# Four row buffers and two moved steps in the last stage of a graph network kernel on one Trainium2 core

## The reference, cut to what matters

```python
proj = (x @ gat_w.T).reshape(n, NH, FOUT)                 # NH 4, FOUT 64
e = jax.nn.leaky_relu(s_src[src] + s_tgt[tgt], 0.2)
exp_e = jnp.exp(e - jnp.max(e))
agg = segment_sum(proj[src] * attn[:, :, None], tgt)      # attn = exp_e / denom[tgt]
...
xc, z = jnp.split(xs @ in_proj_w.T, 2, axis=-1)           # xs: the nodes in order of degree
xc = silu(conv over 4 nodes of xc)
dbc = xc @ x_proj_w.T
dt = softplus(dbc[:, :16] @ dt_proj_w.T + dt_proj_b)
h_t = exp(dt * A) * h_(t-1) + (dt * xc) * B               # 256 channels x 16 states
y = (h @ C + xc * D_param) * silu(z) ; y @ out_proj_w.T
```

## Time and profile before

| what | value |
|---|---|
| median of 3 runs | 8897.01 us (8894.12 to 8900.41) |
| the profiled execution, its own time | 8896.2 us |
| its span | 8894.4 us |
| mean granted clock of PE | 0.724 |
| busy in the span: PE, DVE, ACT, POOL | 52%, 54%, 14%, 58% |
| the last stage | about 6391 to 8387 us of the span |

### The profile page before, as it was taken

How to read it: one execution, slowest core, us unless ns; L and a number is a source line. 1 busy time by engine, 2 the same in 40 slices (tenths; PEclk the granted TensorE clock), 3 DMA queues, 4 the chain that set the end, 5 groups by cost and what they waited for, 6 DMA issues and landing times. The chain is left out here.

```text
span 8894.4 us, 95573 instructions
## 1 busy us (share of the span) xinstructions
PE 4623.8 (52%) x18992; PEld 3629.7 (41%) x18993; DVE 4836.3 (54%) x11590; ACT 1231.8 (14%) x2744; POOL 5163.8 (58%) x4985
## 2 busy tenths in 40 slices
PE   4008244544457777656666555545454555554354
PEld 3002133333356666644444344433344444444333
DVE  9462388888822222245455344444466666666644
ACT  1002011111101111100000000001122222222111
POOL 0021366766667777677777677777655556555400
PEclk6557677677778888877777677777677777667676
DMA  0201256555423333233333233333222332222200
GB/s 8 75 16 52 59 143 170 161 159 162 130 80 94 92 90 94 69 84 99 92 95 95 63 83 96 89 92 92 75 85 83 91 91 83 86 86 80 71 6 9
DMA packets 485777, 772.81 MB, mean 87 GB/s; under 512 B 296031, under 2 KB 316310, under 8 KB 481979
## 3 DMA queue, kind: packets, MB, share of 16 engines
q0 software_dynamic: 265504, 666.90, 27.1%
q10 hardware_dynamic: 19838, 70.21, 2.1%
q1 hardware_dynamic: 200345, 34.81, 2.1%
HBM read 822.37 MB, written 46.03 MB: 98 GB/s over the span
## 5 line engine op out<-in xcount | busy, mean ns | idle before, releaser
L794 POOL DMA_INDIRECT gat_rows<-scratch_gat,gat_index x1856 | 1857.4, 1001 | 576.3 <-issue 540.0
L1071 PE MATMUL gat_ps<-gat_work,k_ident 128*128 128x256 f32 x3712 | 1214.3, 500 | 933.2 <-DVE gat_work L865 817.6
L1645 POOL DMA_INDIRECT m_rows<-scratch_gat,m_index x928 | 1097.1, 1182 | 861.0 <-DVE m_work L1934 581.5
L1071 PEld LDWEIGHTS gat_ps<-gat_work,k_ident 128*128 128x128 f32 x3712 | 941.3, 260 | 1213.2 <-issue 900.4
L794 POOL DMA_INDIRECT conv_rows<-scratch_kv,conv_index x928 | 931.9, 1004 | 410.7 <-issue 267.6
L1071 PE MATMUL conv_ps<-conv_work,k_ident 128*128 128x256 f32 x1856 | 668.4, 538 | 851.2 <-DVE conv_work L865 779.5
L1211 POOL DMA_INDIRECT rel_rows<-scratch_x,rel_index x928 | 926.7, 999 | 286.5 <-issue 273.8
L1071 PEld LDWEIGHTS conv_ps<-conv_work,k_ident 128*128 128x128 f32 x1856 | 511.8, 283 | 1008.2 <-issue 821.2
L1698 PE MATMUL m_ps<-m_work,k_ident 128*128 128x256 f32 x1664 | 524.2, 487 | 359.2 <-DVE m_work L1934 359.2
L1443 PE MATMUL rel_ps<-rel_factor,rel_rows 128*128 128x128 f32 x3712 | 581.6, 330 | 214.6 <-DMA rel_rows<-scratch_x,rel_index 214.6
L1443 PEld LDWEIGHTS rel_ps<-rel_factor,rel_rows 128*128 128x128 f32 x3712 | 563.2, 244 | 226.8 <-DMA rel_rows<-scratch_x,rel_index 154.5
(11 more groups left out here) (453 smaller groups left out, 7840.3 us busy)
## 6 DMA issues: line engine op xcount, KB each, us to landing
m_bc<-scratch_bc ACTq DMA_DIRECT2D x25, 2048.0 KB, 8.6
gat_rows<-scratch_gat,gat_index POOLq DMA_INDIRECT x1856
conv_rows<-scratch_kv,conv_index POOLq DMA_INDIRECT x928
rel_rows<-scratch_x,rel_index POOLq DMA_INDIRECT x928
m_rows<-scratch_gat,m_index POOLq DMA_INDIRECT x928
scratch_runs<-e_runs_sb SPq DMA_DIRECT2D x1, 12890.6 KB
scratch_kv<-p_row ACTq DMA_DIRECT2D x25, 256.0 KB
gat_index<-scratch_slots SPq DMA_DIRECT2D x232, 4.0 KB, 1.8
```

Source lines behind the costliest of these rows:

```text
L794: pool.indirect_dma_start(out=rows[b][:, s, :], out_offset=None, in_=table, in_offset=bass.IndirectOffsetOnAxis(ap=index[b][:, s:s + 1], a ...
L1071: ins = pe.matmul(ps_sum[min(b, 1)], ident, work[b][:, s, :], start=s == 0, stop=s == S - 1)
L1645: pool.indirect_dma_start(out=rows[b][:, s, :], out_offset=None, in_=dr["gat3"], in_offset=bass.IndirectOffsetOnAxis(ap=index[b][:, s:s + ...
```

## The change

A fourth row buffer (with index and extras buffers) is added. The first chunk of a tile now always takes buffer 3 (`FIRST_BUF`), the second takes buffer 2 (`SECOND`, number 4 in the lists, which is buffer 2 again and shares its semaphores with the tails), and the later ones take 0 and 1 in turn, with a tail in 2 as before. The products `work` and the two sum banks keep their turns (first chunk 0, second 1). Two more rows of `sched` and a class `Stay` in place of `Visit` count these uses; PE, DVE, ACT, POOL and SP all use it in this stage.

On ACT, `exp` of the second chunk moves from behind `turn(t + 2)` to ahead of it. On PE, `front(t + 1)` moves from behind `sum_slots` of the first chunk to ahead of it. DVE's order is the same.

```diff
+            st.do(v.tensor_scalar(kp["sched"][:, LATER, 0:T], per[:, 0, :], -2.0, None, ALU.add))
+            st.do(v.tensor_tensor(cum[:, USES, :], cum[:, USES, :], tile_no[:], ALU.subtract))
+            st.do(v.scalar_tensor_tensor(kp["sched"][:, LATER_CODE, 1:T + 1], cum[:, USES, :], float(1 << TAIL_BITS),
                                          cum[:, RECORDS, :], ALU.mult, ALU.add))
...
+FIRST_BUF, SECOND = 3, 4
...
+    def uses(self, j, b):
+
+        if b == TAIL_BUF:
+            return self.tails + self.t + 1
+        return self.t if b == FIRST_BUF else self.tails + self.t if b == SECOND else self.later + j
...
+def stay(eng, w, chunk):
+
+    with eng.If(w.pairs > 0):
+        with eng.Fori(0, w.pairs) as j:
+            chunk(w, j, 0)
+            chunk(w, j, 1)
+    with eng.If(w.tail > 0):
+        chunk(w, w.pairs, TAIL_BUF)
...
-        rows = [sb(f"rows{b}", [P, S, width]) for b in range(3)]
+        for shared in (index_in, extras_in, gathered, released):
+            shared.append(shared[TAIL_BUF])
+        index = [sb(f"index{b}", [P, S], I32) for b in range(4)]
+        extras = [sb(f"extras{b}", [P, S]) for b in range(4)]
+        rows = [sb(f"rows{b}", [P, S, width]) for b in range(4)]
+        for shared in (index, extras, rows):
+            shared.append(shared[TAIL_BUF])
...
             with tile_loop(nc, pool, 0, T) as t:
-                visit(pool, kp, t, gather)
+                w = Stay(pool, kp, t)
+                gather(w, 0, FIRST_BUF)
+                gather(w, 0, SECOND)
+                stay(pool, w, gather)
...
         @block.tensor
...
             def tile(t, has_front, ahead):
-                w = Visit(pe, kp, t)
-                sum_slots(w, 0, 0)
+                w = Stay(pe, kp, t)
                 if has_front:
                     front(t + 1)
+                sum_slots(w, 0, FIRST_BUF)
                 sum_states(t)
                 if ahead:
                     project(t + 2)
-                sum_slots(w, 0, 1)
+                sum_slots(w, 0, SECOND)
                 flow_out(t)
-                rest(pe, w, sum_slots)
+                stay(pe, w, sum_slots)
...
         @block.scalar
...
             def tile(t, has_front, ahead):
...
                 if has_front:
                     write_bc(t + 1)
                     soft(t + 1)
                     spread_bc(t + 1)
+                exp(w, 0, SECOND)
                 if ahead:
                     turn(t + 2)
-                exp(w, 0, 1)
-                if ahead:
                     gates(t + 2)
                 store(t)
-                rest(act, w, exp)
+                stay(act, w, exp)
```

More of the change, by code:

```diff
@@ L663, in chunk, with __init__, read, record @@
         return self.chunks + j * 2 + (0 if b == TAIL_BUF else b)
+FIRST_BUF, SECOND = 3, 4
+class Stay:
+    def __init__(self, eng, kp, t):
+        def read(row, least, most):
+            return eng.value_load(kp["sched"][0:1, row, bass.ds(t, 1)], min_val=least, max_val=most)
+        code = read(LATER_CODE, 0, (CHUNKS_MAX // 2 << TAIL_BITS) + T)
+        later = read(LATER, 0, E // S + 2)
+        self.t, self.later = t, code >> TAIL_BITS
+        self.tails = code & ((1 << TAIL_BITS) - 1)
+        self.pairs, self.tail = later >> 1, later & 1
+        self.records = self.later + self.tails + t
+        self.chunks = self.later + self.records + t
+    def uses(self, j, b):
+        if b == TAIL_BUF:
+            return self.tails + self.t + 1
+        return self.t if b == FIRST_BUF else self.tails + self.t if b == SECOND else self.later + j
+    def chunk(self, j, b):
+        if b >= FIRST_BUF:
+            return self.chunks + (b - FIRST_BUF)
+        return self.chunks + j * 2 + (2 if b == TAIL_BUF else 2 + b)
+    def record(self, j, b):
+        if b >= FIRST_BUF:
+            return self.records * 2 + (b - FIRST_BUF)
+        return (self.records + j) * 2 + (2 if b == TAIL_BUF else 2 + b)
+def bank_of(b):
+    return (0, 1, 1, 0, 1)[b]
+def stay(eng, w, chunk):
[5 more added lines that the diff above has]
+        chunk(w, w.pairs, TAIL_BUF)
 def visit(eng, kp, t, chunk, in_first=None):
@@ L1526, in attend_and_scan @@
         index_in, extras_in, gathered, released = (
-            [sem(f"{n}{b}") for b in range(3)] for n in ("index_in", "extras_in", "gathered", "released"))
+            [sem(f"{n}{b}") for b in range(4)] for n in ("index_in", "extras_in", "gathered", "released"))
         zeroed, pace, begun, g_steps = sem("zeroed"), sem("pace"), sem("begun"), sem("g_steps")
@@ L1806, in _ @@
             G_PER, G_PRO, G_END = 11, 3, 2
-            for b in range(3):
+            for b in range(4):
                 v.sem_inc(released[b], 1)
@@ L1930, in weigh @@
                 n, c = w.uses(j, b), w.chunk(j, b)
-                first = isinstance(j, int) and b == 0
-                second = isinstance(j, int) and b == 1
+                first, second = b == FIRST_BUF, b == SECOND
                 v.wait_ge(probs_ready, c + 1)
@@ L1996, in chunk @@
                     v.sem_inc(begun, 1)
-                rest(v, w, chunk)
-                g = Steps(v, g_steps, t * (G_PRO + G_END - 1) + G_PRO - 1 + w.chunks_end * G_PER)
+                stay(v, w, chunk)
+                g = Steps(v, g_steps, t * (G_PRO + G_END - 1) + G_PRO - 1 + (w.chunk(w.pairs, TAIL_BUF) + w.tail) * G_PER)
                 g.add(v.tensor_copy(tile_of(kp["den"], t), den[:]))
```

54 lines of the change are left out of this document (27 added, 27 removed).

## The result

The changed kernel takes 8654.89 us (median of 4 runs, 8654.47 to 8655.75) against 8896.03 of the kernel before beside it (4 runs). The ratio is 0.9728, 95% interval 0.9715 to 0.974. The forecast was 8656, 1.1 us too much. The profiled execution has a span of 8652.7 us, 241.7 under that of before.

A forecast was written before the change was run, and what follows sets the result against it. DVE, which every other engine waits for, was taken to bound the last stage, shortened by what DVE's waits lose. The sum was 8896.2 - 130 - 103 - 23 + 16 = 8656 us, range 8622 to 8708.

The forecast's parts named there:

- The second exponential: ACT, tiles 0 to 22: exponential ahead of the copy cuts waits 150.6 to 6.2 us, 14 lost at projection; gain 130.
- The third exponential: DVE's wait for the third chunk's exponential, 3.56 us in tile 10: left unchanged, swinging 0.5 us a tile with PE's clock.
- The front ahead of the slot sum: PE, 24 tiles: DVE's wait at the `m_dbc` copy falls to 0.65 us each (bounds 0.4 and 0.85); gain 103 us.
- The fourth buffer: First chunks of tiles 4 to 23: 31.0 us of row waits go, a 0.4 us gap stays of each; gain 23.
- Buffer 2 in the last tiles: Tiles 23 and 24: second chunk and tail share buffer 2, so the tail's rows come late; loss 16 us.
- Costed at nothing: Later slot sums, the fourth buffer's memset and priming transfer, and four tiny DVE operations in `fetch_nodes`: no time.
- DVE is not held by gathers: Rival: short DVE steps each wait for the gather under way, 15 us a tile, giving 9001 us, slower; 2%.
- POOL did not become the bound: Rival: POOL bounds tiles 3 to 12, rows 5 us late in 10 tiles, giving 8706 us; 7%.
- PE's sum of states: Rival: at PE's lower clock the sum sets the pace, up to 2 us more wait a tile, giving 8696 us; 12%.
- The rival of a fourth buffer that does nothing: Rival: SP loads indices strictly in order and stands at the tail's release, giving 8679 us; 8%.
- its terms (6, 14 and 12 us): Low end of the range: `m_dbc` waits 6 us either way, no projection wait 14 less, third exponential's wait 12 either way.

The follow-up runs named there:

- the kernel with the sixth entry: Changed kernel with ACT's store behind the later chunks' exponentials and, in tiles of 3 chunks, the tail in buffer 0: 8585.67 us, ratio 0.9653.

## Why the prediction was right

- *The second exponential.* Forecast 130 us, of them 144.4 from the waits and 14 given back. The waits fell by just that, every second weighing waits 0.3 us, and 16.6 came at `m_seq`. Right in place and size. Alone it brought 144.6, more than forecast: the next point gives 10.7 of it, `m_acc` 11.0, and of the 14 for `m_seq` only 9.5 came.
- *The third exponential*, which the prediction left as it was (3.56 us in tile 10) with a swing for PE's clock of 0.5 us a tile, gained 11.2 us. Before, it stood at 2.6 or 3.6 us by tiles; after, at 2.6 in all. Where it is 3.54 the output product took 2.08 us, and 1.13 where it is 2.62 and in the changed kernel. In tile 10 PE now idles only 1.41 us ahead of that product (4.94 before), and the granted clock over it is 1.00 (0.50 before). The exponential's move alone does this (61.2 us of waits), the front's does not (78.5). This is the term that the sum lacked.
- *The front ahead of the slot sum.* Forecast 103 us, measured 94.8. The mis-sized term is the wait with PE free, taken at 0.65 us between bounds of 0.4 and 0.85: it is 0.99, above both. In tile 10 the product itself takes 1.08 us, not 0.64, under a granted clock of 0.50 instead of 1.00: PE comes to it after 6.15 us of idling, where before it came straight from the slot sum. Taking 0.64 from the row behind a busy PE was the mistake; the row before tile 0, with 0.85 and a product of 1.09 us at 0.50, was nearer. The 0.14 us that it lacks stay open.
- *The fourth buffer.* Forecast 23 us in tiles 4 to 23, measured 31.0 - 10.7 - 4.6 = 15.7. The mis-sized term is the gap that stays, taken at 0.4 us a tile behind `m_own`: it is 0.5 to 0.6 us there, and two others grow beside it. With the loss in the last tiles nothing is left, and the buffer alone did bring nothing. On top of both moves it brought about 8 us, as the forecast's 23 - 16 = 7 has it, but for another reason: with three buffers the shorter tiles would have waited 38.5 us for rows and not 31.0, and `m_dbc` and other waits for PE are some 5 us less with it.
- *Buffer 2 in the last tiles.* Forecast waits 7.4, 2.8 and 9.2 us; measured 7.89, 3.07 and 9.84. The way from release to rows in use, 12.8 us by tile 10's rows, was 12.65 us in tile 23 (second weighing's end at 8067.81, tail at 8080.46) and 12.16 in tile 24, so it was not too short. DVE came to the tails 0.6 and 1.3 us sooner than forecast, since the gaps and a wait for states that stood ahead of them before are now part of the longer wait. Less what they cover, the loss is 15.5 us, as the forecast's 16.
- *Costed at nothing*: the wait for the slot sum fell by 6.9 us (in tile 10 the sums of the third and fourth chunk took 9.26 us together, where they took 10.09). The stage begins 0.3 us later, so that the fourth memset and the small index work can't be told from the spread of that start over the kernels. The 2.6 us by which the end of the program is longer I did not look into.
- *The rivals.* DVE is not held by gathers: the scan took 4.42 us with a gather of 4.65 beside it in both halves of a tile. The Trainium skill ("SBUF — State Buffer", Who interferes with whom) says of DVE's two-port modes that the one that starts first blocks the other for its whole instruction, and that issue order decides who blocks. Taken for the scan, that fits the gather at 7193.20, which starts 0.58 us after the scan and lasts to 7197.85, 0.8 us past the scan's end. It does not fit the reverse: the gather of 7190.51 runs for 2.39 us, to 7192.90, and the scan that begins under it at 7192.62 takes its 4.42 us all the same. So do all others: 47 of the 50 scans of the changed kernel begin under a gather, 22 of the kernel before have none beside them, and each of the 100 lasts 4424 to 4426 ns. By the rule DVE would have lost time at such places; the scans lost none. POOL did not become the bound, but it came near: it is idle 3.82 us in a tile of 5 chunks of 68.3 us, and the 64.5 us between are the prediction's figure. PE's sum of states did take part in setting the pace: in tiles 14 to 22 it took 6.4 to 6.75 us instead of 5.4, and `m_seq` waits 1.1 to 1.5 instead of 0.2 us. That rival had been priced at 40 us; it cost some 11, inside the 16.6. The rival of a fourth buffer that does nothing came true for the buffer alone, but by the gaps and the last two tiles and not, as it said, by SP's order: the rows of tiles 4 to 22 were no longer waited for.

The sum was right to 1 us because its errors cancel. The gain was 8.2 us less than forecast at `m_dbc`, 2.6 at `m_seq`, 2.7 behind `m_own`, 4.6 at the two other gaps and 2.9 outside the stage, 21.0 together. It was 11.2 us more at the third exponential, 6.9 at `m_acc`, 1.2 at the first tiles' rows, 0.5 in the last tiles and 2.5 in small waits, 22.3 together. The terms were off by up to 11 us; an error of 1 us in all is luck. The range has a slip: its terms (6, 14 and 12 us) give 8624 for the low end, not 8622.

## What to carry over

In the list of an engine that others wait for, put the short step whose input is ready ahead of the one that waits, then ask what stands ahead of the next short step: here the same question asked once more (the store ahead of the third exponential) brought another 58 us. A buffer removes waits, but what it is worth is what is left after the gaps that show once they are gone: here 31.0 us of waits went and 30.8 came in other places. Which chunks share a buffer is a choice: not the first chunk and the tail ahead of it, at 8.4 us a tile of 5 chunks, where sharing between the second chunk and the tail cost 15.5 us in two tiles. Take the duration of a step that will follow an idle engine from a row where it follows one, not from a row behind busy work.

## What was not expected of the hardware

- PE's short steps differ by nearly 2 with the granted clock that they meet: the 4 products of L1732 take 1.08 us at 0.50, after 6.15 us of idling, and 0.64 at 1.00, right behind the slot sum; the output product takes 2.08 us at 0.50 or 1.13 at 1.00; the states, which meet both levels, 6.67 to 6.77 or 5.43 to 5.61, with no edit to them. The granted clock of the stage rose from 0.72 to 0.75. Such differences repeat from tile to tile for nine or ten tiles on end, so a small gain can be enlarged or taken back in every one of them.
- The hold of DVE on a gather goes one way: gathers 1.00 us alone, 4.55 to 4.66 under a scan, and the scan 4.42 in either case. In the changed kernel the 928 gathers take 1223.2 us against 1097.1 before, and in tiles 4 to 22 DVE waits for no rows all the same.
- A few branches and register reads a tile cost DVE some 0.3 us (8 us over 25 tiles at the two lines shown, in the kernel with the sixth entry); that the edit's branches are the cause is not tested alone.
